# A fused graph and attention layer: GpSimd zeroes the graph weight's sums, and the second row tile is loaded and normalised ahead of the weight parts

## The reference

```
xn = layernorm(x)
# graph part: the edges are the nonzeros of a 1024 x 1024 weight W, which they build by a scatter-add
W = zeros(1024, 1024).at[src, dst].add(edge_weight)       # indices outside are dropped
g = xn @ W.T + gnn_bias
# linear attention, 16 heads of 64, one sequence of 1250 rows
q, k, v = split(xn @ W_qkv)
q, k = relu(rmsnorm(q, qn_w)), relu(rmsnorm(k, kn_w))
kv = sum over rows of k^T v (by head);  norm = q . sum(k) + 1e-6
a = (q @ kv / norm) @ W_out + b_out
x1 = x + g + a
# mixture of 8 experts, top 2, on rmsnorm(layernorm(x1)); clipped swiglu, hidden 256
out = x1 + layernorm(x1) + moe(...)
```

## Time and profile before

| | |
|---|---|
| three timed runs | 1002.86, 1008.80, 1009.12 us, median 1008.80 |
| the profiled execution | 1005.02 us |
| its span, first to last instruction | 1003.3 us, so 1.7 us lie around it |
| mean granted TensorE clock | 0.97 of full |
| busy: TensorE / VectorE / ScalarE / GpSimd | 918.4 / 724.9 / 366.5 / 170.4 us |
| the first stage, row tiles 0 and 1 | 0 to about 79 us |
| GpSimd, first constants to its next instruction | idle for 292.1 us, until 296.6 us |

### The profile page before, as it was taken

How to read it: one execution, slowest core, us unless ns; L and a number is a source line. 1 busy time by engine, 2 the same in 40 slices (tenths; PEclk the granted TensorE clock), 3 DMA queues, 4 the chain that set the end, 5 groups by cost and what they waited for, 6 DMA issues and landing times.

```text
span 1003.3 us, 16230 instructions
## 1 busy us (share of the span) xinstructions
PE 918.4 (92%) x5361; PEld 574.4 (57%) x5362; DVE 724.9 (72%) x1213; ACT 366.5 (37%) x621; POOL 170.4 (17%) x210
## 2 busy tenths in 40 slices
PE   4897999999998999998999999999479899999993
PEld 3555766766765654555666666666445455455551
DVE  5777999999999984267877888866845455555551
ACT  5748666666441215331112222222123233233331
POOL 1000000000000000003331332322112233333322
PEclk9998999999999999999999999999689999999996
DMA  9744667666663008921145555566589959885544
GB/s 307 233 142 135 206 214 217 188 191 189 223 209 129 22 23 188 329 72 42 59 138 168 156 163 154 149 177 181 209 291 312 298 125 280 264 261 125 125 84 63
DMA packets 89162, 176.59 MB, mean 176 GB/s; under 512 B 24824, under 2 KB 39160, under 8 KB 89088
## 3 DMA queue, kind: packets, MB, share of 16 engines
q1 hardware_dynamic: 81328, 147.50, 46.7%
q0 software_dynamic: 7776, 28.32, 12.8%
HBM read 113.63 MB, written 62.67 MB: 176 GB/s over the span
## 4 chain that ended last, share of the span: by engine, by line
PE 37%; DVE 28%; DMA 15%; issue 7%; ACT 7%; POOL 3%; SPq 2%; DVEq 1%; POOLq 0%; ACTq 0%
PE windows L1055 9%; PE bank L921 7%; DMA arena<-t_dram,arena 6%; PE bank L771 5%; DMA arena<-in_w_flat 4%; PE bank L1073 4%; DVE arena L1710 3%; DVE arena L1534 3%; DVE arena L1544 3%; PE bank L953 2%; DMA out_x<-arena 2%; PE bank L1046 2%; DMA split_dram<-arena 2%; DVE arena L1813 2%; DVE arena L1521 1%
## 5 line engine op out<-in xcount | busy, mean ns | idle before, releaser
L771 PE MATMUL bank<-arena 128*125 128x512 f16 x960 | 217.1, 383 | 7.0 <-DVE arena L1502 4.0
L771 PEld LDWEIGHTS bank<-arena 128*125 128x125 f16 x960 | 130.5, 138 | 80.8 <-DVE arena L1502 4.4
L1055 PE MATMUL windows<-arena 128*128 x648 | 150.2, 382 | 0.1
L921 PE MATMUL bank<-arena 128*128 128x416 f16 (+1 forms) x576 | 107.3, 342 | 2.1 <-DMA arena<-split_dram 2.1
L1055 PEld LDWEIGHTS windows<-arena 128*128 128x128 f16 x648 | 63.9, 99 | 66.3 <-issue 2.7
L947 PE MATMUL bank<-arena 128*125 128x512 f16 x432 | 96.2, 379 | 1.6 <-ACT arena L1305 1.6
L953 PE MATMUL bank<-arena 128*125 128x512 f16 x432 | 95.8, 379 | 0.0
L921 PEld LDWEIGHTS bank<-arena 128*128 128x128 f16 x576 | 55.5, 98 | 46.8 <-DMA arena<-split_dram 2.5
L1813 DVE SCALAR_TENSOR_TENSOR arena<-arena 128x512 f16<-128x512 f32 x40 | 51.3, 1287 | 39.2 <-ACT arena L1344 39.0
L947 PEld LDWEIGHTS bank<-arena 128*125 128x125 f16 x432 | 58.8, 137 | 35.0 <-issue 2.3
L953 PEld LDWEIGHTS bank<-arena 128*125 128x125 f16 x432 | 59.0, 137 | 33.4
(11 more groups left out here) (254 smaller groups left out, 1421.8 us busy)
## 6 DMA issues: line engine op xcount, KB each, us to landing
arena<-split_dram SPq DMA_DIRECT2D x56, 512.0 KB, 6.8
arena<-in_w_flat SPq DMA_DIRECT2D x44, 512.0 KB, 4.5
split_dram<-arena SPq DMA_DIRECT2D x88, 256.0 KB, 4.7
arena<-in_w_flat SPq DMA_DIRECT2D x40, 256.0 KB, 4.2
split_dram<-arena SPq DMA_DIRECT2D x80, 128.0 KB, 2.4
arena<-in_x SPq DMA_DIRECT2D x20, 448.0 KB
arena<-in_w_qkv SPq DMA_DIRECT2D x8, 1024.0 KB, 10.4
t_dram<-arena SPq DMA_DIRECT2D x10, 448.0 KB
```

The source lines that it names most:

```text
L771: mm = pe.matmul(bank[b][0:TT, :], xt[:, l, k, tok(i)], wkv[:, r, k, c0:c0 + 512], start=(k == 0 and n == 0), stop=(k == KT - 1 and n == 2))
L921: mm = pe.matmul(bank[u % 3][:, 0:n], wq[h][:, l, k, :], xt[:, r, k, a:a + n], start=(k == 0 and c == 0), stop=(k == KT - 1 and c == 2))
L1055: mm = pe.matmul(bank[6][:, :], rowT[s][:, l, k, :], arena16[:, bass.ds(off + (r * KT + k) * 512, 512)], start=(k == 0 and c == 0), stop=( ...
```

## The change

Three edits. First, the eight zeroings of `w_acc` go from ScalarE to GpSimd, as eight memsets behind a wait for `table_done`. GpSimd has nothing else to do there, and its next instruction in order is the wait of L632. ScalarE's `zero_windows(0)` now comes ahead of `v_half(1, 1)`. Second, the loads of row tile 1 are issued right behind those of row tile 0, ahead of all weight parts. Third, the normalisation steps of row tile 1 are moved forward on both engines: `row_sums(1)` ahead of `wkv_part_hi(0)`, `row_variance(1)` ahead of `wkv_part_lo(0)`, `row_root(1)` and `row_scale(1)` behind part 0, `row_norm(1)` behind part 3 and ahead of part 4. ScalarE's wait for `row_sq` ahead of `k_square(0, 0)` goes.

```diff
             load_x(0)
+            load_x(1)
             load_wkv(0)
             load_wkv(1)
             load_wkv(2)
             load_wkv(3)
             sp.dma_start(knw, kn_w.partition_broadcast(P)).then_inc(knw_in, 16)
-            load_x(1)
...
             pool.wait_ge(consts, 11)
+            pool.wait_ge(table_done, 1)
+            for k in range(KT):
+                pool.memset(w_acc[:, k * D:(k + 1) * D], 0.0).then_inc(acc_zero, 1)
...
             first_sqrt()
+            row_sums(1)
             wkv_part_hi(0)
+            row_root(1)
             for half in range(2):
                 xt_hi_half(0, half)
             for m in (1, 2, 3):
                 wkv_part_hi(m)
-            row_sums(1)
+            row_norm(1)
             wkv_part_hi(4)
-            row_root(1)
-            a_.wait_ge(row_sq, 2)
             k_square(0, 0)
             wkv_part_hi(5)
-            row_norm(1)
             k_relu(0, 0)
...
-            def zero_sums(k):
-                a_.activation(w_acc[:, k * D:(k + 1) * D].rearrange("p (a b) -> p a b", b=P), zeros.unsqueeze(1).to_broadcast([P, KT, P]), ACT.Copy).then_inc(acc_zero, 1)
...
             a_.wait_ge(table_done, 1)
-            for k in range(2):
-                zero_sums(k)
+            zero_windows(0)
             v_half(1, 1)
-            zero_windows(0)
-            for k in range(2, KT):
-                zero_sums(k)
             piece_hi(halves(2)[0])
...
             first_norm()
+            row_variance(1)
             wkv_part_lo(0)
+            row_scale(1)
             for half in range(2):
                 xt_lo_half(0, half)
             for m in (1, 2, 3):
                 wkv_part_lo(m)
-            row_variance(1)
-            row_scale(1)
             wkv_part_lo(4)
```

## The result

The change makes the kernel 0.6% faster: ten runs with a median of 999.8 us (997.8 to 1002.8) against ten of before with 1005.3, ratio 0.9943 with a 95% interval of 0.992 to 0.9965, or 5.7 us (3.5 to 8.0 by the interval's ends). The profiled execution took 997.8 us with a span of 996.0. The forecast was 6 us. The total held, but two of the three terms of its sum didn't.

A forecast was written before the change was run, and what follows sets the result against it. TensorE was taken as the bound behind 95.9 us, with idle times of 6.2 us ahead of steps(1) and 3.0 ahead of unit 2 to save. 3.55 + 1.6 + 0.9 = 6.05 us from 1006.9 gave 1001, range 995 to 1007.

The forecast's parts named there:

- Part one: Zeroing on GpSimd lets k_weighted(2, 0) start at 83.3 us instead of 86.86, gaining 3.55 us.
- The clock: With shorter idle time ahead of steps(1), TensorE's clock was to stay up behind it, gaining 1.6 us.
- I take the upper level: Choice that TensorE's clock stays up behind 2.6 us of idle time: 1.6 us gained, 0 the other end.
- rival two: TensorE's clock falls again behind the idle time ahead of steps(1): 4.4 us gained, 1002.5 us; chance 0.27.
- The likeness to the full load ahead of the 3.0 us in the head: Full TensorE work ahead of steps(1) resembles that ahead of unit 2's 3.0 us idle, where granted clock was 1.00.
- Part two: Row tile 1's loads and normalisation ahead of the weight parts: low part 4 at 26.6 instead of 27.52, gaining 0.9 us.
- so I leave its landing at 24.65: Weight part 4 still lands at 24.65 us, since the same bytes precede it and the queue holds work.
- Rival four: Weight parts 4 to 7 land with their issue: 1.1 us lost instead of 0.9 gained, 1003 us; chance 0.11.
- TensorE is still ready when low part 4 is: In the head, TensorE's units 0 and 1 come 2.0 us later, but the 3.0 us idle behind them covers it.
- They are hidden in ScalarE's wait for part 0: Row tile 1's 3.0 us of sums on ScalarE finish before weight part 0 lands at 11.3 us.
- Rival three: GpSimd memsets and VectorE makes block each other, so memsets run behind make(1): 1.3 us slower, 1008 us; chance 0.08.
- Rival five: VectorE becomes the bound or a later wait takes the gain: within 2 us of before, 1006 us; chance 0.12.

The follow-up runs named there:

- e4_wait_late: Changed kernel with VectorE's wait for the zeroing moved from ahead of row tile 2 to right ahead of accumulate(0); median 997.6 us, ratio 0.9908 to the kernel before.
- e1_pool_zero: Kernel before with only the zeroing moved to GpSimd memsets and zero_windows(0) put ahead of v_half; ratio 0.995 to the kernel before.
- e10_all: Changed kernel with the late zeroing wait, make(1) behind k_weighted(2, 0) and 48 zero-tile matmuls ahead of unit 0; median 998.4 us, ratio 0.9904 to before.
- e6_apart: Kernel before with the knw broadcast issued behind weight part 4, row tile 1's loads left behind part 3; ratio 0.9989 to the kernel before.
- e3_load_only: Kernel before with only row tile 1's loads moved right behind row tile 0's, no engine steps moved; ratio 0.9959 to the kernel before.
- e5_again: Changed kernel run once more, unedited; ratio 0.9932 to the kernel before.

## Why the prediction was right

The forecast was 1001 us and 6 us gained; 999.8 us and 5.7 us were measured. Most of the 1.2 us between 1001 and 999.8 is the time of before, taken as 1006.9 and measured as 1005.3. The three terms of the gain were 3.55, 1.6 and 0.9.

**Part one, 3.55 us: right, step by step.** The eight memsets took 7.17 us (7.2 forecast), VectorE stood 1.49 us for them (1.3), the idle time was 2.73 and 2.68 us (2.6), from `k_weighted(2, 0)` to `steps(1)` passed 6.4 us. Alone it moved `k_weighted(2, 0)` by 3.5 us from `table_done`. e4_wait_late showed that the memsets' pace was what was late next, and that nothing but the place of VectorE's wait made it so.

**The clock, 1.6 us: wrong.** "I take the upper level" failed. Behind 2.7 us of idle time the granted clock was 0.50, in the changed kernel, in its second run and in e1_pool_zero, as rival two had it. The likeness to the full load ahead of the 3.0 us in the head decided nothing. Behind 1.15 us (e4_wait_late) and 0.54 us (e10_all) it stayed up: the unit took 5.34 us.

**Part two, 0.9 us: too small by more than half in the profiled run, 2.5 us at `table_done`.** The step that failed is "so I leave its landing at 24.65". It counted the row tile's bytes as equal wherever they stand in the queue. They aren't: in the middle they went at 242 to 287 GB/s with the DMA engines fully busy (242 in e6_apart, 261 before, 287 in e1_pool_zero), where weight parts went at 390. At the start they cost less than the 1.7 us forecast: ScalarE took up part 2, at its landing, at 15.82 (15.59 in e3_load_only) in place of 15.00, so 0.6 to 0.8 us later. By 7 us 183 GB/s had flowed on average where 192 had before. Part 4 landed 2.1 us sooner, at 22.55, and not at 24.65. With the 0.9 us of the moved steps that is the 3.0 us at low part 4. Rival four, the landing tied to the issue, fell with it: part 4 was issued at 14.95 and landed 7.6 us behind, not 10.8. (Its loss of 1.1 us was read at high part 4; counted at low part 4, as the 0.9 us were, it would have been 0.7.)

**"TensorE is still ready when low part 4 is": wrong.** Unit 0 started 1.4 us later, not 2.0, but low part 4 came 3.0 us earlier. The bound of the head went over to TensorE, which worked on without a break past that point, and with it the time until TensorE is at full pace: 17.3 or 18.3 us for the same 72 matmuls. "They are hidden in ScalarE's wait for part 0" failed too, by up to 0.5 us: part 0 landed at 10.2 to 10.5 (e3_load_only, e5_again), not at 11.3, and the sums of row tile 1 ran until 10.80. At the stage's end part two measured 0.7 us alone, and 1.4 and 2.3 in the two runs of the changed kernel against e1_pool_zero. TensorE's pace explains 0.7 us of that spread, the store of a piece 0.5; the rest is open.

**Rival three** (memsets and makes hold each other up) fell: both kept their times. With copies in place of the memsets the makes were held up, and `steps(1)` came 4.0 us later, but there the copies' own 1.49 us each ended last. **Rival five** fell: 6.35 us were there at the end of the first stage.

So the total was right because an error of 1.6 us one way and one of about 1.6 the other cancelled in the profiled run. That was luck. In the second one, e5_again, `table_done` came 1.8 us earlier than before, and 5.4 us were there at the stage's end.

## What to carry to other kernels

When a wait for a batch of preparation stands ahead of a whole loop, put it ahead of the first instruction that reads the result; here that was worth 2.6 to 2.8 us more from `table_done` to the end of the stage, part of it because the clock stayed up. A zeroing went well on GpSimd beside VectorE as a memset, and badly as a copy. And the position of a transfer in a queue isn't only a matter of bytes: read the rate by the microsecond, and try the slow one where the queue isn't full yet. What is moved ahead of the first unit has a price there: the loads alone won as much as loads and steps together.

## What the hardware showed that I had not expected

The transfer of one row tile of 125 rows of 4 KB brought the rate down to 242 to 287 GB/s at a DMA share of 1.03 or 1.04, beside weight parts in pieces of 2 KB at 386 to 391. Row size alone isn't the reason, since the broadcast of `knw`, also 4 KB to each of 128 partitions, went through at 390 in the changed kernel. The cause stays open.

The granted clock reads 1.00 in the stretches from 14 to 20 us in all twelve profiles, though without the 48 matmuls the first weight loads of unit 0 stood 0.43 us apart there, twice the 0.22 of later ones. In the head the pace of the matmuls has to be read, not the clock's column.

SyncE's issue of the `knw` broadcast took 4.4 us before and 3.8 after, against 0.4 us of an ordinary one, with everything behind it in SyncE's order waiting. It is the place and not the broadcast that does it. In e6_apart the two loads of row tile 1 stand there, behind four weight parts, and take 5.2 us together, while `knw` takes 0.5 behind part 4:
```profile
4.21 5.20 SPq L397 DMA_DIRECT2D arena<-in_x  x2
...
14.44 0.51 SPq L449 DMA_DIRECT2D arena<-in_kn_w  x1
```
